# Moving the first feed-forward units of a Transformer block in front of the last attention step's transposes

## What is computed

```python
x = x + _layernorm(attn(_layernorm(x)))   # 16 heads of 8, causal, relative positions -2..2
x = x + _layernorm(ffn(_layernorm(x)))

# ffn, for every token
shared = silu(xf @ sw1) * (xf @ sw3) @ sw2          # 128 -> 256 -> 128
s = sigmoid(xf @ router_w.T)                        # 8 experts
_, topk_idx = top_k(s + router_bias, 2)             # two are chosen
gates = s_sel / (s_sel.sum() + 1e-9)
h = gelu(einsum('nd,edh->neh', xf, ew1)); y = einsum('neh,ehd->ned', h, ew2)
out = shared + einsum('ned,ne->nd', y, comb)        # comb: gates at the chosen experts
```

## Time and profile before

| | |
|---|---|
| median of 3 runs | 1051.91 us (1050.83 to 1052.38) |
| the profiled execution's own time | 1049.69 us |
| its span in the trace | 1048.0 us |
| busy: TensorE / VectorE / GpSimd / ScalarE | 910.0 (87%) / 837.1 (80%) / 729.3 (70%) / 675.1 (64%) us |
| TensorE clock granted, mean | 0.956 of full speed |
| chain that ended last: PE / DVE / POOL / ACT / issue | 44% / 18% / 12% / 12% / 6% |

### The profile page before, as it was taken

How to read it: one execution, slowest core, us unless ns; L and a number is a source line. 1 busy time by engine, 2 the same in 40 slices (tenths; PEclk the granted TensorE clock), 3 DMA queues, 4 the chain that set the end, 5 groups by cost and what they waited for, 6 DMA issues and landing times.

```text
span 1048.0 us, 23476 instructions
## 1 busy us (share of the span) xinstructions
PE 910.0 (87%) x7655; PEld 521.8 (50%) x7655; DVE 837.1 (80%) x1948; ACT 675.1 (64%) x1303; POOL 729.3 (70%) x940
## 2 busy tenths in 40 slices
PE   2768889999999999899999999987289999999995
PEld 0334444444444444444444444432167777777774
DVE  5677888888888988888888888974478887878874
ACT  2137677677767776776777777665047767676773
POOL 4135586876966867768769668555448889898886
PEclk9869999999999999999999999988589999999998
DMA  2610110110101101101101011020325454555540
GB/s 49 167 45 31 35 44 32 45 43 30 51 32 40 47 33 43 45 32 46 42 32 51 31 42 46 22 67 19 100 91 149 154 160 142 168 155 166 163 137 31
DMA packets 64004, 74.93 MB, mean 72 GB/s; under 512 B 10032, under 2 KB 39600, under 8 KB 63904
## 3 DMA queue, kind: packets, MB, share of 16 engines
q1 hardware_dynamic: 61536, 73.17, 22.1%
q10 hardware_dynamic: 2368, 0.48, 0.3%
HBM read 43.75 MB, written 8.65 MB: 50 GB/s over the span
## 4 chain that ended last, share of the span: by engine, by line
PE 44%; DVE 18%; POOL 12%; ACT 12%; issue 6%; SPq 5%; DMA 1%; POOLq 0%; DVEq 0%; ACTq 0%
PE ps_av L1532 10%; DVE mx L1114 7%; PE ps_av L1731 6%; ACT prob L792 6%; POOL prob L634 5%; PE ps_s L1698 5%; PE ps_e L1472 5%; SPq L454 5%; PE ps_misc L1540 4%; PE ps_s L1495 3%; PE ps_e L1698 3%; POOL hidden_low L735 2%; ACT av_s L857 2%; PE ps_s L1516 2%; DVE hidden_low L1368 2%
## 5 line engine op out<-in xcount | busy, mean ns | idle before, releaser
L1114 DVE TENSOR_REDUCE mx<-ps_s 128x1 f32<-128x512 f32 (+2 forms) x640 | 409.4, 684 | 78.3 <-PE ps_s L1516 75.5
L792 ACT ACTIVATE prob<-ps_e 128x512 f32<-128x512 f32 x640 | 347.4, 601 | 118.8 <-PE ps_e L1472 118.8
L634 POOL TENSOR_SCALAR_AFFINE_SELECT prob<-prob 128x516 f32<-128x516 f32 (+1 forms) x320 | 173.1, 565 | 170.0 <-ACT prob L792 170.0
L1495 PE MATMUL ps_s<-ks,qs 63*128 63x512 f16 (+3 forms) x1024 | 214.7, 311 | 21.0 <-DMA ks<-kl 8.3
L1472 PE MATMUL ps_e<-qs,ks 64*128 64x512 f16 (+3 forms) x1024 | 196.5, 303 | 14.7 <-DMA qs<-mT 7.1
L735 POOL TENSOR_TENSOR hidden_low<-hidden,hidden_high 128x512 fp32r<-128x512 f32 x144 | 191.4, 1357 | 20.3 <-ACT hidden_high L981 19.0
L1532 PE MATMUL ps_av<-prob,vp 128*32 128x512 f32 (+3 forms) x2048 | 182.6, 452 | 23.2 <-POOL prob L634 23.0
L981 ACT CAST hidden_high<-hidden 128x512 fp32r<-128x512 f32 x160 | 98.1, 613 | 34.8 <-DVE hidden L1420 30.7
L1472 PEld LDWEIGHTS ps_e<-qs,ks 64*128 64x128 f16 x1024 | 60.8, 95 | 115.5 <-ACT prob L792 64.0
L1516 PE MATMUL ps_s<-masked_at,below_r 64*128 64x128 bf16 (+3 forms) x640 | 106.4, 211 | 0.0
L1495 PEld LDWEIGHTS ps_s<-ks,qs 63*128 63x128 f16 x1024 | 63.5, 94 | 79.6 <-DVE mx L1114 54.9
(11 more groups left out here) (175 smaller groups left out, 1745.0 us busy)
## 6 DMA issues: line engine op xcount, KB each, us to landing
gate_rows<-gates_dram SPq DMA_DIRECT2D x128, 256.0 KB, 3.6
qs<-qh SPq DMA_DIRECT2D x128, 32.0 KB
qs<-ql SPq DMA_DIRECT2D x128, 32.0 KB
xnT_dram<-oT SPq DMA_DIRECT2D x16, 256.0 KB, 2.0
xeT<-xnT_dram SPq DMA_DIRECT2D x16, 256.0 KB, 2.7
out<-result SPq DMA_DIRECT2D x16, 256.0 KB, 2.3
v_near<-v_back SPq DMA_DIRECT2D x16, 254.0 KB
ks<-kh SPq DMA_DIRECT2D x124, 32.0 KB
```

What stands on the lines that cost most here:

```text
L634: pool.affine_select(out=v, in_=v, compare_op=ALU.is_ge, fill=0.0, base=-2, pattern=cols, channel_multiplier=-1).then_inc(S["p_masked"], 1)
L792: act.activation(prob[g % 2][:, u, b, :], ps_e[bank][:, :], ACT.Exp, scale=SCALE).then_inc(S["e_done"], 1)
L1114: dve.tensor_reduce(out, src, AX.X, ALU.max).then_inc(s_free[bank], 1)
L1495: pe.matmul(scores[:, at:at + P * (qt + 1)], qs[par][rows, 2 * g + off, P * qt:P * qt + P], ks[par][rows, 2 * g + off, 0:P * (qt + 1)], st ...
```

## The change

**What it does.** Five first products of sequence 0 (`FIRST = 5`: c0, e0, e1, e2, c1) and the second product of c0 are put in front of the last step's `xn2` transposes on TensorE (`first_units`); they wait for `y_out` to have emptied `ps_s2`, no more for the logits. ScalarE's part of the five units goes in front of `xn2T_out`, VectorE's part of the first four in front of `x1_bn`, and GpSimd's first `low_half` in front of the second `normalise`. The weight splits and the first row split go into VectorE's part of the last step, around `av_tok_out(3)`. On SyncE's queue both row loads go behind four of the eight gate loads, and the last sequence's store to DRAM behind the first feed-forward sequence's gate loads. The transpose of the late gates goes from unit 1 to unit 3 of sequence 1, their copy behind `end_out`.

```diff
+FIRST = 5
...
                     for e in range(NE):
                         load_gate(0, e)
-                    sp.wait_ge(S["av_full"], NGRP * NSEQ)
-                    sp.wait_ge(S["xnT_stored"], 16 * (NSEQ - 1))
-                    load_xe(0, 0)
-                    load_xe(1, 1)
+                        if e == NE // 2 - 1:
+                            sp.wait_ge(S["av_full"], NGRP * NSEQ)
+                            sp.wait_ge(S["xnT_stored"], 16 * (NSEQ - 1))
+                            load_xe(0, 0)
+                            load_xe(1, 1)
...
+                if f.s0 == 0:
+                    rows_out(Step(NSEQ + 2))
+                    sp.wait_ge(S["xnT_stored"], 16 * NSEQ)
...
                 masks(12, 15)
+                if st.t0 == NSEQ + 2:
+                    low_half(Ffn(0), 0)
                 if st.C:
                     normalise(st, st.c, xn2[:, :, :], tiles(xr[:, st.c, :]), mv3, var3, rs3,
                               "stats3").then_inc(S["xn2_ready"], 1)
...
+                if st.t0 == NSEQ + 2:
+                    ffn_part(Ffn(0), 0, FIRST)
                 if st.C:
                     xn2T_out(st)
...
-                    if i == LAG - 2 and f.s0 == 1:
+                    if i == LAG - 1 and f.s0 == 1:
                         gates_out(False)
...
+                if st.t0 == NSEQ + 2:
+                    split_weights()
                 if st.C:
                     av_tok_out(st, st.c, 3)
+                if st.t0 == NSEQ + 2:
+                    dve.wait_ge(S["av_full"], NGRP * NSEQ)
+                    split_second_weights()
+                    split_rows_high(Ffn(0), 0)
+                    split_rows_low(Ffn(0), 0)
...
+                if st.t0 == NSEQ + 2:
+                    ffn_part(Ffn(0), 0, FIRST - 1)
                 if st.C:
                     x1_bn(st)
                     aggregate(st3, mv3, "stats3")
...
+                    if f.s0 == 0 and i == LAG:
+
+                        dve.wait_ge(S["misc_free"], Step(NSEQ + 2).misc("logits") + 1)
...
+            def first_units(st):
+
+                pe.wait_ge(S["w_split"], 1)
+                pe.wait_ge(s_free[st.s_use("oproj")[1]], st.s_turn("oproj") + 1)
+                for i in range(FIRST):
+                    first(Ffn(0), i)
+                    if i >= LAG:
+                        second(Ffn(0), i - LAG)
...
+                            if st.t0 == NSEQ + 2 and what == "xn2":
+                                first_units(st)
                             use()
...
-                    pe.wait_ge(S["misc_free"], Step(NSEQ + 2).misc("logits") + 1)
-                for i in range(n):
+                for i in range(FIRST if f.s0 == 0 else 0, n):
                     first(f, i)
                     if i == LAG and f.s0 > 0:
                         end_transpose(f, -1)
-                    if f.s0 == 1 and i == 1:
+                    if f.s0 == 1 and i == LAG - 1:
                         gate_transposes(False)
```

More of the change, by code:

```diff
@@ L967, in step @@
                     first_keys()
-            steps(act, step)
             def end_out(f, s):
@@ L981, in high_half, with ffn_part @@
                 act.copy(hidden_high[hid(f, i)][:, :].bitcast(F32R), hidden[hid(f, i)][:, :]).then_inc(S["high_ready"], 1)
-            def ffn(f):
-                if f.s0 == 0:
+            def ffn_part(f, lo, hi):
+                if f.s0 == 0 and lo == 0:
                     act.wait_ge(S["av_full"], NGRP * NSEQ)
-                for i, (kind, k) in enumerate(UNITS):
+                for i in range(lo, hi):
+                    kind, k = UNITS[i]
                     if kind == "c":
@@ L1338, in step @@
                     bias_out()
-            steps(dve, step)
             def end_stats(f, s):
@@ L1401, in _, with ffn_part @@
             late_parts = {(0, 4): gates_scores, (0, 6): gates_second, (0, 8): gates_shares}
-            def ffn(f):
-                own2.begin_ffn(f)
-                if f.s0 == 0:
-                    dve.wait_ge(S["av_full"], NGRP * NSEQ)
-                for i, (kind, k) in enumerate(UNITS):
+            def ffn_part(f, lo, hi):
+                if lo == 0:
+                    own2.begin_ffn(f)
+                for i in range(lo, hi):
+                    kind, k = UNITS[i]
                     dve.wait_ge(S["act_ready"], f.at(i + 1, len(UNITS)))
@@ L1431, in ffn @@
                         end_scale(f, -1)
-                own2.end_ffn(f)
-            split_weights()
-            split_rows_high(Ffn(0), 0)
-            split_rows_low(Ffn(0), 0)
-            dve.wait_ge(S["av_full"], NGRP * NSEQ)
-            split_second_weights()
-            dve.wait_ge(S["misc_free"], Step(NSEQ + 2).misc("logits") + 1)
+                if hi == len(UNITS):
+                    own2.end_ffn(f)
+            def ffn(f):
+                ffn_part(f, FIRST - 1 if f.s0 == 0 else 0, len(UNITS))
+            steps(dve, step)
             ffn_steps(dve, ffn)
@@ L1685, in _ @@
-            pe.wait_ge(S["const_ready"], N_POOL_CONST)
-            steps(pe, step)
             def first(f, i):
```

108 lines of the change are left out of this document (56 added, 52 removed).

## The result

| | before | change |
|---|---|---|
| median of 4 runs, side by side | 1052.09 us (1050.83 to 1052.38) | 1040.09 us (1038.87 to 1040.69) |
| ratio, 95% interval | | 0.988 [0.9867, 0.9893] |
| profiled execution, its span | 1049.69, 1048.0 us | 1038.87, 1037.1 us |
| busy: TensorE / VectorE / GpSimd / ScalarE | 910.0 / 837.1 / 729.3 / 675.1 us | 907.4 / 834.9 / 726.3 / 678.6 us |

The change makes the kernel 12.0 us faster; 1039.9 was predicted. That the two agree to 0.2 us is partly luck: the four runs of the change span 1.8 us, and two later sets of runs have medians of 1038.4. The work is the same (ScalarE has two table loads more), so the gain is idle time. The windows show it (columns as in the earlier trace rows); the first row is the stretch from y_out to the transposes.

A forecast was written before the change was run, and what follows sets the result against it. TensorE bounds the feed-forward loop, so time won ahead of it counts fully. Late gates 11.7 us earlier, e4's hidden values 11.7 to 11.9, taken as 12.0: 1049.69 - 12.0 = 1037.7 profiled, 1039.9 median; range 1037.0 to 1043.9.

The forecast's parts named there:

- TensorE-bound loop, gain one to one: Feed-forward loop, TensorE busy 212.70 of 218 us: whatever is won or lost ahead of it moves the end one to one.
- Splits cost nothing, rows 0.5 us late: Last attention step: splits hide behind TensorE's two last attention products; row loads landing about 741.2 delay y_out by 0.5 us.
- Units take 8.8 us, x1_bn behind them: Ahead of x1_bn: first product to xe_low's end takes 8.8 us; x1_bn at 751.5 waits about 2.9 us.
- Second norm 3.7, not 7.7: GpSimd's second norm, without the weight splits beside it, takes 3.7 us instead of 7.7; xn2 ready at 756.6.
- 4.1 us to the gates, gates 11.7 earlier: Transposes and logits take 4.1 us after the second norm; late gates begin at 760.7 against 772.38, 11.7 us earlier.
- Hidden of e4 11.7 to 11.9 earlier: Behind the gates' start: e4's hidden values at 765.2 by VectorE, 765.0 by TensorE, against 776.89 before.
- From there the same, the gates' transpose moved for nothing (0 to 0.4): Behind e4: same order to the last sequence; moving the late gates' transpose gives nothing to 0.4 us, taken as nothing.
- second norm blocked: Rival, 4%: VectorE work still blocks GpSimd's second norm, which stays at 7.7 us; 1043.9 us in total.
- TensorE at the lower clock: Rival behind the logits: all 42 products slow lose 7.3 us, 1047.2; partly 4%, no change 3%, slower 3%.
- Faster still: Rival, 15%: transposes and logits at the higher clock, 1.5 us less; with rows on time, 1037.0 us.

The follow-up runs named there:

- two like traces: The second and third traces of the unaltered changed kernel; from the last attention step's first normalisation to the end 303.41 and 303.40 us.
- Experiment 3: Changed kernel with both row loads back behind all eight gate loads: stretch from last attention step's first normalisation to end 2.6 us longer than in the two like traces.
- experiment 5: Changed kernel with x1's statistics ahead of the low part of sequence 1's rows: 302.66 us from the last attention step's first normalisation to the end.
- experiment 4: Changed kernel with the second weights' split moved back behind x1's statistics, beside the second norm: late gates 1.6 us later, tail 1.9 us longer.
- first trace: The changed kernel's first profiled execution, no edit: span 1037.1 us, 302.55 us from the last attention step's first normalisation to the end.
- change_third: Third trace of the unaltered changed kernel: 303.40 us from the last attention step's first normalisation to the end.
- experiment 7: Changed kernel with the late gates' transpose back at its old place, twice (tails 305.13, 304.49 us), then with nine surplus products in its wait (`rest` 275.62).
- experiment 6: Changed kernel with twenty surplus products between c0's second product and the transposes: 0.9 us less tail than the two like traces.
- gates_back: Changed kernel with the late gates' transpose back in unit 1 of sequence 1: tails 305.13 and 304.49 us in two traces.
- rows_ninth: Changed kernel with both row loads behind all eight gate loads as before: median 5.2 us above that of the unaltered change, tail 2.6 above.

## Why the prediction was right, step by step

Times behind num; in brackets those of the two like traces of the change.

- **TensorE-bound loop, gain one to one**: from the gates' start to the end it took 275.70 us before and [275.63, 275.70]. Right.
- **Splits cost nothing, rows 0.5 us late**: w_low and o_tok did not move anything. y_out predicted to end at 9.8, [9.40, 9.31], where before had 9.31. The rows held y_out up by 0 to 0.1, not 0.5: a term mis-sized by 0.4, because they landed 7.3 to 7.5 behind num and not the 8.4 (741.2) that was worked out. Experiment 3 shows that the wait is priced one to one if it comes.
- **Units take 8.8 us, x1_bn behind them**: first product to the end of xe_low [8.84, 8.84]; x1_bn predicted at 18.7, [18.25, 18.17], behind xe_low and not GpSimd. Right, and experiment 5 took 0.6 off it. Its wait was 2.2 us and not 2.9; the prediction had moved y_out by 0.5 and not x1_ready, which hangs on it.
- **Second norm 3.7, not 7.7**: GpSimd's four operations take 3.5 us (753.75 to 757.29 in the first trace). Right; experiment 4 gives the other case.
- **4.1 us to the gates, gates 11.7 earlier**: predicted at 27.9, [27.78, 27.70], so [11.70, 11.78] earlier. Right.
- **Hidden of e4 11.7 to 11.9 earlier**: before it stood at 44.07, now [32.21, 32.12]: 11.9. Right, but TensorE's part of it by luck. Its nine products were to take 3.6 us from 27.9 on, six at the lower clock and three at the higher. All nine ran at the lower, 4.2 us, and began 0.6 earlier (760.19 to 764.38 in change_third), so they end where they were forecast.
- **From there the same, the gates' transpose moved for nothing (0 to 0.4)**: the sum of this step is right by luck, and its working is wrong. In the changed kernel the moved transpose saves 1.3 us (experiment 7), three times the upper bound given. In before the old place had cost no clock (1.00 behind the wait at 785.81), but another stretch ran at 0.50 (778.30). The change no longer has that one and has one at the gates' start instead. That the two weigh the same, so that `rest` comes out as in before, is inferred and not shown. The prediction read the 2.08 us of wait at 785.81 as all that the old place could cost, and did not ask what the clock does behind a wait that the change makes longer (2.5).
- **Rivals**: *second norm blocked* did not occur. *TensorE at the lower clock* occurred for ten products behind the logits (760.19 to 764.60 in change_third) and not for all 42, and the tail shows nothing of its 7.3 us. *Faster still* did not occur as named: the transposes and logits stayed at the lower clock, and with the gap filled (experiment 6) they gave 0.8 and not 1.5. The first trace, whose tail is 0.9 shorter, has an earlier cause: its oproj and c0 ran at the higher clock. The Trainium skill (TensorE: Matmul & The Clock Gate, HAM oscillation) warned that idleness costs the clock. The runs agree for the gap of 5 us ahead of the transposes and for the wait of 2.5 us in gates_back, with 0.50 behind both. The prediction priced the first and not the second, and the second decided a part of the diff.

What stays open: the medians of the change (12.0, 12.3 and 12.6 us below before) rest on runs that spread over several us, and before has one trace only, so its tail may be off by as much as the change's traces differ, 0.9. The splits' share of the gain is 1.8 us by the medians and 3.5 by a trace. What the lower clock at the gates' start costs by itself was not isolated, since every kernel with units ahead starts the late gates at it; that it weighs as much as before's stretch at 778.30 is inferred from the `rest` values. Why oproj's clock differs from run to run was not tried.

## What to carry to other kernels

When independent work can be put into a wait, count what is left of the wait afterwards: here 6.5 us of VectorE's remained, and filling 5 of them gave 3.9 us more in the tail. Where a change makes the engine that bounds the rest reach some operation earlier than its input, look at the granted clock behind that wait, not at the wait alone. And where runs of one kernel spread more than a part is worth, compare traces from a common event just ahead of the change.

## What the runs showed of the hardware

- A wait's length alone does not tell whether TensorE's clock falls behind it. It was 1.00 behind waits of 1.70 (change) and 2.08 us (before, 785.81), and 0.50 for about 3 us behind 2.52, 2.53 and 3.63 us. In before it also fell behind one of 1.75 (777.03), about 1.3 us after work had resumed.
- A small VectorE operation can take six times as long beside GpSimd. The late gates' first operation (128x64) took 0.20 us in the change, where GpSimd was idle, and 1.14 in the chain of before, beside GpSimd's low half. In the change's traces xe_low (128x512) took 0.69 alone and 1.50 beside GpSimd's hidden_low (first trace).
- The exponential's table load costs nothing where ScalarE waits anyway: 759.16 + 1.28 ends while the logits run until 761.07.
- Behind four gate loads the two row loads took a median of 4.8 to 5.8 us from issue to landing, and the first split that waited for them started 7.0 to 7.9 us behind num. Behind all eight they took 7.5 in before and 6.4 in `rows_ninth`, where that split started at 10.3.
